# First phase of an AdaLN transformer block: queries and keys laid out by halves of the heads

## The reference, cut to what matters

```
h  = layernorm(x) * (1 + ca) + sa
xn = layernorm(h) * ln_g + ln_b
q, k, v = (xn @ W.T split in heads of d = 32)
x1, x2 = first 16 and last 16 of a head's columns
q = q * cos + concat(-x2, x1) * sin        # k alike; cos and sin repeat after 16 columns
scores = q @ k.T / sqrt(32) ...
qp = q[..., :3] @ head_dirs ; kp = k[..., :3] @ head_dirs
```

## Time and profile before

| | |
|---|---|
| median of 3 runs | 2733.17 us |
| the profiled execution's own time | 2730.83 us |
| its span in the trace | 2729.1 us |
| granted TensorE clock, mean | 0.969 |
| busy: PE, DVE, ACT, POOL | 93%, 80%, 58%, 20% |

### The profile page before, as it was taken

How to read it: one execution, slowest core, us unless ns; L and a number is a source line. 1 busy time by engine, 2 the same in 40 slices (tenths; PEclk the granted TensorE clock), 3 DMA queues, 4 the chain that set the end, 5 groups by cost and what they waited for, 6 DMA issues and landing times. The chain is left out here.

```text
span 2729.1 us, 45326 instructions
## 1 busy us (share of the span) xinstructions
PE 2551.3 (93%) x14104; PEld 1541.0 (56%) x14104; DVE 2171.9 (80%) x4588; ACT 1589.6 (58%) x3509; POOL 554.8 (20%) x404
## 2 busy tenths in 40 slices
PE   7998999999999999996999999799989999997998
PEld 3444333333333333344777777578767777775877
DVE  5988999999999999975888888555658887885665
ACT  3443666666767766653666666544446666664442
POOL 1111011011100111035333333100033333331000
PEclk8997999999999999998999999999989999998999
DMA  3344354545445445453000000220020000001121
GB/s 131 118 133 125 102 133 114 131 122 149 115 110 130 121 126 135 128 177 106 16 17 15 21 16 15 64 89 22 2 63 9 8 9 8 10 16 43 46 68 40
DMA packets 124741, 204.95 MB, mean 75 GB/s; under 512 B 22736, under 2 KB 71952, under 8 KB 121280
## 3 DMA queue, kind: packets, MB, share of 16 engines
q1 hardware_dynamic: 111856, 170.39, 22.2%
q0 software_dynamic: 8688, 21.27, 2.8%
q10 hardware_dynamic: 4080, 11.86, 1.2%
HBM read 125.44 MB, written 54.13 MB: 66 GB/s over the span
## 5 line engine op out<-in xcount | busy, mean ns | idle before, releaser
L1084 ACT ACTIVATE probs<-st_ps 128x512 f32<-128x512 f32 (+3 forms) x640 | 339.0, 530 | 298.7 <-PE st_ps L1013 164.3
L1137 DVE SCALAR_TENSOR_TENSOR geo_x<-geo_rows,kp_t 128x512 f32<-128x512 f32 (+3 forms) x640 | 436.9, 706 | 3.8 <-ACT probs L1086 3.7
L1116 DVE TENSOR_REDUCE chunk_max<-a_ps 128x1 f32<-128x512 f32 (+3 forms) x640 | 358.6, 601 | 37.1 <-PE a_ps L996 31.7
L1086 ACT ACTIVATE probs<-geo_x 128x512 f32<-128x512 f32 (+3 forms) x640 | 360.7, 564 | 12.8 <-DVE geo_x L1143 12.8
L1417 PE MATMUL local_in_ps<-w_local,local_ht 128*128 128x512 f32 x1152 | 321.7, 416 | 9.4 <-ACT local_sq L1559 5.3
L1578 ACT ACTIVATE local_probs<-local_s_ps,local_bias,local_inv 128x256 f32<-128x256 f32 x512 | 282.6, 563 | 13.8 <-DVE local_bias L1673 13.8
L1585 ACT ACTIVATE local_pt<-local_pt_ps 128x512 f32<-128x512 f32 x256 | 152.3, 596 | 209.0 <-PE local_pt_ps L1475 200.7
L1028 PE MATMUL o_ps<-probs,vx_first 128*33 128x512 f32 (+3 forms) x1280 | 274.0, 550 | 0.0
L1856 PE MATMUL ff_ag_ps<-ff_ht_parts,w 128*128 128x512 f32 (+1 forms) x1056 | 255.4, 400 | 17.5 <-DVE ff_gate L1965 9.3
L1028 PE MATMUL o_ps<-probs,vx_ 128*33 128x512 f32 (+3 forms) x1280 | 270.3, 544 | 0.0
L1669 DVE TENSOR_REDUCE local_top<-local_s_ps 128x4 f32<-128x1024 f32 x128 | 156.7, 1224 | 120.9 <-PE local_s_ps L1461 120.9
(11 more groups left out here) (197 smaller groups left out, 4216.9 us busy)
## 6 DMA issues: line engine op xcount, KB each, us to landing
geo_rows<-geo SPq DMA_DIRECT2D x64, 512.0 KB, 7.6
piece_lo<-in_pieces POOLq DMA_DIRECT2D x15, 768.0 KB, 5.7
weight_parts<-piece_hi SPq DMA_DIRECT2D x15, 768.0 KB, 3.4
weight_parts<-piece_lo SPq DMA_DIRECT2D x15, 768.0 KB, 6.0
raw<-out_t SPq DMA_DIRECT2D x128, 64.0 KB
shares_in<-shares SPq DMA_DIRECT2D x64, 128.0 KB, 4.9
q_first<-q_parts SPq DMA_DIRECT2D x24, 256.0 KB, 4.1
k_first<-k_parts SPq DMA_DIRECT2D x24, 256.0 KB, 6.3
```

Source lines behind the costliest of these rows:

```text
L1084: act.activation(probs[:, s % PSLOTS, 0, off:GTOK], st_ps[:, (b * NB + s) % STBANKS, off:GTOK], ACT.Exp).then_inc(q["st_used"], 1)
L1086: act.activation(probs[:, s % PSLOTS, 1, off:GTOK], geo_x[:, s % GSLOTS, off:GTOK], ACT.Exp).then_inc(q["probs_ready"], 1)
L1116: dve.reduce_max(chunk_max[:, it, c:c + 1], a_ps[:, n % ABANKS, 0:width], AX.X).then_inc(q["a_used"], 1)
L1137: ins = dve.scalar_tensor_tensor(out[:, off:GTOK], geo[:, 1, at], kp_t[:, j, ds(b, 1)].rearrange("p o -> p o"), geo[:, 0, at], ALU.add, AL ...
```

## The change

The weights' columns are ordered so that the first 16 columns of all 8 heads come first, then the last 16 of all heads. A bank then holds one half of every head, and the column that a rotation needs stands on the same partition in the other bank. The second product is dropped. The tables shrink to one half (repeated over the heads). The units are now two, queries and keys, each of two banks. The rotation reads the two banks crosswise; a unit takes one instruction of 1024 elements for `rot_c`, two of 512 for `rot_s` and one of 1024 for the sum. `hi` and `lo` are written 1024 at a time. The directions need only the first bank, so one matmul for each. The store of a bank goes to 8 heads x 16 columns. VectorE's and ScalarE's lists are written anew around the two units: `shifted` n + 1 now stands behind both rotations and low part 0; `normed` n + 1 behind both copies of values. SP waits for the queries' parts and stores them, then for the keys'.

```diff
-        self.w = sb("w_qkv", [P, CC, 5 * C])
+        self.w = sb("w_qkv", [P, CC, 3 * C])
...
-                    sp.wait_ge(q["hi_done"], 4 * n + 4 + START)
-                    sp.wait_ge(q["lo_done"], 4 * n + 4 + START)
                     for r, store in enumerate((S.q_parts, S.k_parts)):
+                        sp.wait_ge(q["hi_done"], 2 * n + r + 1 + START)
+                        sp.wait_ge(q["lo_done"], 2 * n + r + 1 + START)
                         for part, tile in enumerate((hi, lo)):
                             for k in range(CC):
-                                dst = store[part, ds(n // GPB * H + k * 4, 4), :, ds(n % GPB * GTOK, GTOK)]
-                                sp.dma_start(dst.rearrange("h d t -> (h d) t"), tile[:, r, k, :].bitcast(F32)).then_inc(q["parts_out"], 16)
+                                dst = store[part, ds(n // GPB * H, H), k * HD:(k + 1) * HD, ds(n % GPB * GTOK, GTOK)]
+                                sp.dma_start(dst, tile[:, r, k, :].bitcast(F32)).then_inc(q["parts_out"], 16)
...
-                        for rot in range(2):
-                            c0 = (u // 2 * 2 + rot) * C + u % 2 * P
+                        for half in range(2):
+                            c0 = u * C + half * P
...
-                        for k in range(CC):
-                            last = pe.matmul(dot_ps[:, :], (dirs_q if u == 0 else dirs)[:, k, :], qk[:, u, k, :],
-                                             start=k == 0, stop=k == CC - 1)
+                        pe.matmul(dot_ps[:, :], (dirs_q if u == 0 else dirs)[:, :], qk[:, u, 0, :], start=True, stop=True).then_inc(q["dot_ready"], 1)
...
-                    dve.scalar_tensor_tensor(rot_c[:, u % 2, :], qk_ps[:, u % 2, 0, :], sc, cos[:, here], ALU.mult, ALU.mult)
-                    last = dve.scalar_tensor_tensor(rot_s[:, u % 2, :], qk_ps[:, u % 2, 1, :], sc, sin[:, here], ALU.mult, ALU.mult)
+                    dve.scalar_tensor_tensor(rot_c[:, :, :], qk_ps[:, u, :, :], sc, cos[:, here].rearrange("p (o t) -> p o t", o=1).to_broadcast([P, 2, GTOK]), ALU.mult, ALU.mult)
+                    dve.scalar_tensor_tensor(rot_s[:, 0, :], qk_ps[:, u, 1, :], -sc, sin[:, here], ALU.mult, ALU.mult)
+                    last = dve.scalar_tensor_tensor(rot_s[:, 1, :], qk_ps[:, u, 0, :], sc, sin[:, here], ALU.mult, ALU.mult)
...
+                    rotate(n, 0)
+                    if more:
+                        modulated(n + 1)
+                    else:
+                        gates(2)
+                    rotate(n, 1)
+                    low_part(n, 0)
+                    if more:
+                        shifted(n + 1)
+                    low_part(n, 1)
                     if not more:
+                        gates(5)
                         dve.tensor_scalar(S.mod[:, 4, :, :], S.mod[:, 4, :, :], 1.0, None, ALU.add)
-                    low_part(n, 3)
```

More of the change, by code:

```diff
@@ L26 @@
 BH = B * H
+HD = D // 2
 EPS = 1e-5
@@ L123, in __init__ @@
         sb, _, sem = allocators(nc, ctx, S.sems)
-        self.w = sb("w_qkv", [P, CC, 5 * C])
+        self.w = sb("w_qkv", [P, CC, 3 * C])
         self.cos, self.sin = sb("cos_t", [P, T]), sb("sin_t", [P, T])
         self.ln_g, self.ln_b = sb("ln_g", [P, CC]), sb("ln_b", [P, CC])
-        self.dirs = sb("dirs", [P, CC, H])
+        self.dirs = sb("dirs", [P, H])
         self.xin, self.xhat = sb("xin", [P, GT, C]), sb("xhat", [P, GT, C])
@@ L167, in _ @@
                 for h in range(H):
-                    sp.dma_start(E.dirs[h % 4 * D:h % 4 * D + 3, h // 4, h:h + 1],
+                    sp.dma_start(E.dirs[h * HD:h * HD + 3, h:h + 1],
                                  io["head_dirs"][:, h:h + 1], allow_slow_non_contiguous=True).then_inc(E.loaded, 16)
@@ L205, in _ @@
                 c = Counter(dve, E.chain, base=0)
-                dve.memset(E.dirs[:, :, :], 0.0).then_inc(E.dirs_zero, 1)
+                dve.memset(E.dirs[:, :], 0.0).then_inc(E.dirs_zero, 1)
                 dve.wait_ge(stage_done, EXP_DONE)
@@ L353, in group @@
                         normalised(n + 1)
[L354 to L357, removed]
+                    for u in range(2):
+                        act.wait_ge(q["rope_done"], 2 * n + u + 1 + START)
                         if u == 0:
                             act.wait_ge(q["parts_out"], 16 * 8 * n + START)
[L360 to L364, removed]
+                        act.activation(hi[:, u, :, :], qk[:, u, :, :], ACT.Copy).then_inc(q["hi_done"], 1)
+                    for u in range(2):
+                        act.wait_ge(q["v_ready"], 2 * n + u + 1 + START)
+                        act.activation(S.v[:, ds(n * GT + 2 * u, 2), :, :],
+                                       v_ps[:, u, :].rearrange("p (t h d) -> p t h d", t=2, h=H), ACT.Copy).then_inc(q["v_used"], 1)
+                    if more:
+                        normed(n + 1)
                     for u in range(2):
@@ L396, in group @@
                     pe.wait_ge(q["xnt_ready"], CC * n + CC + START)
-                    for u in range(4):
-                        pe.wait_ge(q["qk_used"], 4 * n + u + 1 + START)
-                        for rot in range(2):
-                            c0 = (u // 2 * 2 + rot) * C + u % 2 * P
+                    for u in range(2):
+                        pe.wait_ge(q["qk_used"], 2 * n + u + 1 + START)
+                        for half in range(2):
+                            c0 = u * C + half * P
                             for k in range(CC):
-                                last = pe.matmul(qk_ps[:, u % 2, rot, :], w[:, k, c0:c0 + P], xnt[:, k, :],
+                                last = pe.matmul(qk_ps[:, u, half, :], w[:, k, c0:c0 + P], xnt[:, k, :],
                                                  start=k == 0, stop=k == CC - 1)
@@ L413, in group @@
                                 last = pe.matmul(v_ps[:, u, t * C:(t + 1) * C], xnt[:, k, (2 * u + t) * P:(2 * u + t + 1) * P],
-                                                 w[:, k, 4 * C:5 * C], start=k == 0, stop=k == CC - 1)
+                                                 w[:, k, 2 * C:3 * C], start=k == 0, stop=k == CC - 1)
                         last.then_inc(q["v_ready"], 1)
@@ L420, in group @@
                         pe.wait_ge(q["dot_used"], 2 * n + u + START)
-                        pe.wait_ge(q["rope_done"], 4 * n + 2 * u + 2 + START)
-                        for k in range(CC):
-                            last = pe.matmul(dot_ps[:, :], (dirs_q if u == 0 else dirs)[:, k, :], qk[:, u, k, :],
-                                             start=k == 0, stop=k == CC - 1)
-                        last.then_inc(q["dot_ready"], 1)
+                        pe.wait_ge(q["rope_done"], 2 * n + u + 1 + START)
+                        pe.matmul(dot_ps[:, :], (dirs_q if u == 0 else dirs)[:, :], qk[:, u, 0, :], start=True, stop=True).then_inc(q["dot_ready"], 1)
                 pe.wait_ge(E.loaded, E.count)
@@ L466, in rotate @@
                     here = ds(n % GPB * GTOK, GTOK)
[L467 to L470 removed]
+                    sc = 1.0 / math.sqrt(D) if u == 0 else 1.0
+                    dve.wait_ge(q["qk_ready"], 2 * n + u + 1 + START)
+                    dve.scalar_tensor_tensor(rot_c[:, :, :], qk_ps[:, u, :, :], sc, cos[:, here].rearrange("p (o t) -> p o t", o=1).to_broadcast([P, 2, GTOK]), ALU.mult, ALU.mult)
+                    dve.scalar_tensor_tensor(rot_s[:, 0, :], qk_ps[:, u, 1, :], -sc, sin[:, here], ALU.mult, ALU.mult)
+                    last = dve.scalar_tensor_tensor(rot_s[:, 1, :], qk_ps[:, u, 0, :], sc, sin[:, here], ALU.mult, ALU.mult)
                     last.then_inc(q["qk_used"], 1)
[L472 removed]
+                    dve.wait_ge(q["qk_used"], 2 * n + u + 3 + START)
                     if u == 0:
                         dve.wait_ge(q["dot_ready"], 2 * n + START)
[L475 removed]
+                    dve.tensor_tensor(qk[:, u, :, :], rot_c[:, :, :], rot_s[:, :, :], ALU.add).then_inc(q["rope_done"], 1)
                 def low_part(n, u):
[L478 to L480 removed]
+                    dve.wait_ge(q["hi_done"], 2 * n + u + 1 + START)
+                    dve.tensor_tensor(lo[:, u, :, :], qk[:, u, :, :], hi[:, u, :, :].bitcast(F32), ALU.subtract).then_inc(q["lo_done"], 1)
                 def directions(n, first):
@@ L512, in group @@
                         directions(n - 1, first)
[L513 to L520, removed]
+                    rotate(n, 0)
[5 more added lines that the diff above has]
+                    low_part(n, 0)
+                    if more:
+                        shifted(n + 1)
+                    low_part(n, 1)
                     if not more:
+                        gates(5)
                         dve.tensor_scalar(S.mod[:, 4, :, :], S.mod[:, 4, :, :], 1.0, None, ALU.add)
-                    low_part(n, 3)
                 dve.wait_ge(E.loaded, E.count)
-                dve.tensor_scalar(dirs_q[:, :, :], dirs[:, :, :], math.sqrt(D), None, ALU.mult).then_inc(q["qk_used"], 2)
```

(8 more changed lines are left out.)

4 lines of the change are left out of this document (2 added, 2 removed).

## The result

| | before | changed |
|---|---|---|
| median of 4 runs | 2733.60 us | 2788.94 us |
| lowest to highest | 2731.45 to 2739.83 | 2787.39 to 2791.15 |
| ratio of the medians, 95% interval | | 1.0195 (1.0179 to 1.0212) |
| span of the profiled execution | 2729.1 us | 2788.2 us |
| granted TensorE clock, mean | 0.969 | 0.941 |

The change costs 55 us. It was forecast as slower by 30, in a range that ended at 2776; the time lies above it. 48 of the 59 us in the span are in the first phase, 11 in what follows, which the change doesn't touch.

A forecast was written before the change was run, and what follows sets the result against it. The first phase was taken as bound by a ring from VectorE's statistics through V, second root and load. First group 3.5, six rings 25.8 and tail 0.8 gave +30 on 2730.8: 2761 us, range 2749 to 2776.

The forecast's parts named there:

- The ring: First phase, each group: statistics to V, then second root, load, next statistics; forecast 27.3 us for 23.0, six times.
- V: End of the variance row of `shifted` on VectorE; the second root, then the next load's issue, wait for it.
- I take 1.1, landing V + 7.6.: Next rows' load: lands 1.1 us later than V + 6.45, between bounds of V + 6.45 and V + 9.8.
- The hindrance by the stores: Load sharing half its engines with the stores: its 2.4 us of flow lengthens by 0.4 to 1.8, taken as 1.1.
- The root: GpSimd's steps behind V before it issues the next load: load issued at V + 2.07, as before the change.
- The first group: Start of the first phase: first V at 53.8 for 50.35, +3.5 us.
- the tail: From the last V to the first phase's end: 38.1 us for 37.3, +0.8.
- The stores on 8 engines: Stores with outermost count 8 use 8 engines, 190 GB/s; the phase ends 3.6 us later than with 16.
- The load is held until the stores are through: Rival: load lands at V + 9.8, ring 29.5 us, +43 us, 2774; chance 0.1.
- TensorE did go cold: Rival: TensorE stays at half clock in the first phase, ring 29 us, 2773 with a slower tail; chance 0.1.
- The dots' ring: V through `hn`, transposes, key dots and their copy to `directions`: 24.2 us a group; deciding alone, 2742, chance 0.04.
- The savings: First phase, per group: VectorE saves some 1.2 us of work; TensorE's list falls from 23.1 to about 14.4 us.

The follow-up runs named there:

- b_late_shift: Kernel before, with only the order changed: `shifted` behind the fourth rotation, second norm behind both copies of values; 2782.4 us, ratio 1.0188 to before.
- x_order: Changed kernel with `shifted` ahead of the second rotation, and values and second norm ahead of the second `hi`; 2724.4 us, ratio 0.9969 to before.
- x_stores_wait: Changed kernel, with SyncE beginning a group's stores only when the load of the next rows has landed; 2762.3 us, ratio 1.0101 to before.
- x_store16: Changed kernel with columns laid out by half, column, head, so the store's outermost count is 16 instead of 8; 2769.4 us, ratio 1.0145 to before.
- x_order_load: Changed kernel with x_order's order and the load of the next rows issued behind the first root; 2724.3 us, ratio 0.9969 to before.
- x_delay: Changed kernel with four idle memsets of 128x512 on VectorE at the start of the first phase; 2785.2 us, ratio 1.0199 to before.
- x_load_early: Changed kernel, with GpSimd issuing the load of the next rows behind the first root, ahead of the second; 2760.7 us, ratio 1.0113 to before.
- x_all: x_order_load plus the column layout of x_store16, so stores spread over 16 engines; 2714.9 us, ratio 0.9937 to before.

## Why the prediction was wrong, step by step

*The ring.* Right. V, second root, load, statistics set the group's length, six times, with the idle time and its cause as foretold. From statistics to V 19.7 was forecast and 19.8 measured. b_late_shift and x_order show that the order carries the loss, from both sides.

*"I take 1.1, landing V + 7.6."* This step failed, and with it the range. The landing was V + 10.4, even past the upper bound of 9.8. Two terms were mis-sized:

- The hindrance by the stores: forecast 1.1 (0.4 to 1.8), measured 3.0 (from issue 7.40 against 4.38 before; x_stores_wait takes it back to 4.52). The bound of V + 9.8 took the stores to be over at V + 9.2. They were issued more slowly (112.53 to 120.89 for the eight, where 126.53 to 131.01 did before) and flowed until about V + 13, so that all of the load's flow lay beside them. The load alone isn't slack either, as the prediction had it ("doesn't fill the engines alone"): in the kernel before, with only the load in flight, the share reaches 1.03 and 426 GB/s:

```profile
124.50:125.00 0.50, 0.33 (x2) 0.06 (x1) 0.33 (x1) 0.50 (x2) 0.00 (x0) 1.00 1.03 426
```

  An estimate from these figures: an even share on the eight engines in common would at most double the 2.4 us of flow and cost 2.4. Measured were 3.0; why it is more is not shown.
- The root. The 2.07 us from V to the issue were taken as fixed. They hold a GpSimd instruction whose length depends on what VectorE does beside it: 1.01 with a rotation out of PSUM (before, and x_order), 1.38 with a low part of 0.69, 1.91 with one of 1.22. The move itself changed the neighbour. The Trainium skill, "SBUF — State Buffer", section "SBUF: two separate sides", has the rule: VectorE with two inputs from SBUF and GpSimd reading SBUF take one port pair in turn, each for a whole instruction. The trace agrees, nearly: by the rule a root that waits for the low part would end 1.01 behind it, and beside either low part it ends 0.86 behind. With the rule the forecast would have had some 1.0 us a group more.

Together they make the group 30.0 instead of 27.3: 16 us of the 29 by which the profiled execution, at 2789.9, lies above the forecast. The first group and the tail add 1.7, and the part behind the phase 11. Without these 11 the time would be about 2778, still just above the range.

*The stores on 8 engines.* Right: share 0.5, and the tail 38.8 for 38.1 (x_store16's is 3.8 shorter, for 3.6 forecast). Beyond the tail the count is worth 1.0 us a group in the changed order, and in x_order_load it holds up `hi`.

*The first group.* V at 54.8 for 53.8; 0.6 of it is there before TensorE's first transposes (32.26 for 31.62).

*What follows the phase.* The prediction counted nothing for it, "since nothing outside it is touched": it was +11.2 us. The 200 us of the attention phase in the middle, before, and the same work in the changed kernel:

```profile
600.00:800.00 200.00, 191.51 (x916) 75.67 (x917) 189.47 (x382) 134.47 (x291) 22.64 (x24) 0.97 0.50 134
```

```profile
652.00:855.00 203.00, 194.21 (x905) 77.28 (x905) 189.38 (x379) 133.39 (x285) 21.91 (x24) 0.94 0.52 132
```

VectorE has the same work and TensorE a lower clock. Time and again in this phase the granted clock falls to half for 3 to 7 us: behind the phase's start 14 times in the changed kernel and 11 in the kernel before. Summed over stretches of 5 us as (1 - clock) x 5, 980 us from the first phase's end lose 51.0 us in the changed kernel and 34.5 to 39.5 in the kernel before and the nine others here. So the one kernel with the long rest is the one with the large sum; that the sum makes the 11 us is not shown. Nor is it enough that the phase starts late: in b_late_shift it starts later still, at 279.6, and the rest is 2503.8. That the exact start decides is a reading that the profiled execution of x_delay fits; what places the drops stays open.

*The rivals.* "The load is held until the stores are through" (0.1) came nearest, with the group at 29.5, but not for its reason: the load landed ahead of the stores' end, and 0.9 us is the root's. TensorE did go cold, from 113 to 123 in the group shown, but closed no ring. The dots' ring, priced at 24.2 and 6.6 us behind V, is really 26.7 and 9.15 (x_load_early): the root takes 1.93 there, and TensorE is at half clock, which the prediction had counted as 8.5.

*The savings.* VectorE's list without its waits fell from about 21.7 us a group to 20.7 (x_all), 1.0 where 1.2 was forecast. TensorE was busy 22.3 us a group before and 17.1 in the changed kernel; the 14.4 of the forecast was for full clock, and the clock was 0.73. x_all shows what the change is worth where the load closes no ring: 23.0 to 21.05 a group, half of it saved work and half waits that are gone.

## What to carry to other kernels

Before work is moved in an in-order list, find the point that releases the slowest hand-over (here the variance that lets a DMA be issued) and add up what stands behind it: saved work turned into idle time because two rotations went from behind that point to ahead of it. A latency that a trace shows hidden and alone isn't a constant: ask which transfers and which neighbour engine will run beside it in the new order. Give a store an outermost count that 16 divides, and where a load closes the ring, issue it as soon as its buffer is free (the phase ends 21 us earlier here; in the kernel before, where it cost no time, nothing is won).

## What the runs showed of the hardware that was not expected

- A GpSimd instruction of four elements a partition lasts 1.01 to 1.91 us, by what VectorE runs beside it, and that stands in the way of a load that it precedes.
- A load of 512 KB that is in use 4.4 us from its issue when alone takes 7.4 beside stores that use half of the engines, and 6.3 beside stores that use all.
- The same instructions behind the first phase took 11 us more in the changed kernel than in the one before, with TensorE's granted clock at 0.94 instead of 0.97 in the stretch shown. The cause isn't shown.
